# The first layer's front re-ordered: context loaded early, the sum with the summary made in TensorE's accumulators, constant transposes between short products, the one-hot table in halves

## The reference, cut to what matters

```python
def _L0_xattn_ref(Z, kv, decay, W_in, b_in, W_out, b_out, gamma, beta):
    K = jax.nn.sigmoid(decay)
    x = jnp.einsum('btd,ed->bte', kv, W_in) + b_in
    def scan_fn(s, xt):
        s = K * s + xt
        return (s, s)
    _, states = lax.scan(scan_fn, s0, jnp.swapaxes(x, 0, 1))
    proj = jnp.einsum('btd,ed->bte', states, W_out) + b_out
    summary = jnp.mean(proj, axis=1, keepdims=True)
    y = Z + summary
    return (y - mu) / jnp.sqrt(var + LN_EPS) * gamma + beta

x = x + _L0_xattn_ref(_layernorm(x), ctx_2048, ...)   # kv is (4, 64, 256)
x = x + _L0_ffn_ref(_layernorm(x), ...)               # 32 experts, 6 per token, 96 slots each
...
```

## Time and profile before

| | |
|---|---|
| median of 3 runs | 1086.76 us (1084.02 to 1087.8) |
| profiled execution, its own time | 1086.69 us |
| its span | 1085.4 us |
| PE busy | 949.7 us, 87% |
| DVE busy | 741.5 us, 68% |
| ACT busy | 637.0 us, 59% |
| POOL busy | 518.0 us, 48% |
| mean granted TensorE clock | 0.958 of full |

### The profile page before, as it was taken

One profiled execution on the slowest core, in us unless ns is written; L12 is line 12 of the kernel. 1 busy time (PEld: TensorE's weight loads), 2 busy tenths in 40 slices (PEclk: granted clock), 3 DMA queues, 4 the chain that ended last, 5 costly groups with the idle time before them and its releaser, 6 DMA issues.

```text
span 1085.4 us, 18121 instructions
## 1 busy us (share of the span) xinstructions
PE 949.7 (87%) x5833; PEld 786.0 (72%) x5833; DVE 741.5 (68%) x1996; ACT 637.0 (59%) x1816; POOL 518.0 (48%) x579
## 2 busy tenths in 40 slices
PE   6989871989987957599999999999999989997997
PEld 5776551565875756588898889888988778686785
DVE  6563222766664468689898989888888598668344
ACT  2655521020342537689898889989888663653353
POOL 1417773446544643255555555555443155543453
PEclk9789996999998989899999999999999999998999
DMA  9507987500036760020202020202000081005774
GB/s 386 190 18 210 219 212 191 152 1 0 2 137 219 252 218 1 1 64 2 64 2 64 2 63 2 64 1 64 14 13 2 1 251 28 1 1 214 240 272 164
DMA packets 57326, 108.57 MB, mean 100 GB/s; under 512 B 13648, under 2 KB 35280, under 8 KB 55312
## 3 DMA queue, kind: packets, MB, share of 16 engines
q1 hardware_dynamic: 47984, 89.42, 24.8%
q0 software_dynamic: 9248, 18.00, 6.4%
HBM read 78.67 MB, written 27.42 MB: 98 GB/s over the span
## 4 chain that ended last, share of the span: by engine, by line
PE 44%; DVE 19%; ACT 14%; DMA 8%; issue 7%; POOL 7%; SPq 1%; ACTq 0%; DVEq 0%; POOLq 0%
PE bank L201 22%; PE bank L210 7%; ACT a_p L3069 4%; DMA sum<-f_ys,f_index 4%; ACT a_p L3077 3%; PE bank L1338 3%; PE bank L2619 2%; PE bank L1872 2%; ACT a_qt L3052 2%; POOL f_xs L2190 2%; DVE a_qn L2828 2%; DVE stats L240 2%; ACT a_p L3019 1%; POOL sum L1199 1%; PE bank L2669 1%
## 5 line engine op out<-in xcount | busy, mean ns | idle before, releaser
L3196 POOL TENSOR_TENSOR a_p<-a_p,a_tot 128x128 f32<-128x128 f32 x64 | 50.6, 809 | 182.2 <-DVE a_tot L2800 182.2
L201 PE MATMUL bank<-a_w_high,a_in 128*128 128x256 f32 x384 | 99.1, 296 | 13.5 <-ACT a_p L3077 5.0
L210 PE MATMUL bank<-const 128*128 128x128 f32 x433 | 61.4, 300 | 43.1 <-DVE x L1111 21.4
L201 PE MATMUL bank<-a_w_low,a_in 128*128 128x256 f32 x384 | 94.8, 285 | 0.0
L210 PEld LDWEIGHTS bank<-const 128*128 128x128 f32 x433 | 55.8, 157 | 47.5 <-DVE x L1111 21.8
L201 PEld LDWEIGHTS bank<-a_w_high,a_in 128*128 128x128 f32 x384 | 74.1, 193 | 15.9 <-ACT a_p L3077 5.2
L3069 ACT ACTIVATE a_p<-bank,a_top 128x256 f32<-128x256 f32 x128 | 59.0, 477 | 31.0 <-DVE a_top L2852 28.6
L201 PEld LDWEIGHTS bank<-a_w_low,a_in 128*128 128x128 f32 x384 | 74.2, 193 | 0.0
L2852 DVE TENSOR_REDUCE a_top<-bank 128x2 f32<-128x512 f32 (+1 forms) x96 | 57.1, 601 | 20.3 <-PE bank L2619 15.6
L201 PE MATMUL bank<-cols,a_kv 128*128 128x256 f32 x256 | 61.9, 385 | 3.1 <-ACT a_kv L2992 3.1
L201 PE MATMUL bank<-a_proj_high,a_catq 128*128 128x256 f32 x256 | 62.5, 285 | 1.2 <-DVE a_catq L2247 0.8
(11 more groups left out here) (442 smaller groups left out, 3008.1 us busy)
## 6 DMA issues: line engine op xcount, KB each, us to landing
experts<-in_experts SPq DMA_DIRECT2D x49, 384.0 KB, 4.6
f_expert<-in_experts SPq DMA_DIRECT2D x31, 384.0 KB, 5.7
third_shelf<-in_groups SPq DMA_DIRECT2D x8, 1024.0 KB, 6.3
f_got<-f_xs SPq DMA_DIRECT2D x10, 516.0 KB, 8.0
third_shelf<-in_groups SPq DMA_DIRECT2D x8, 512.0 KB, 4.1
f_got<-f_ys SPq DMA_DIRECT2D x8, 512.0 KB, 5.2
f_xs<-blank_zero SPq DMA_DIRECT2D x1, 3999.0 KB, 21.6
l_expert<-in_experts SPq DMA_DIRECT2D x10, 384.0 KB, 7.7
```

The lines of the kernel that those rows point to most:

```text
L201: ins = pe.matmul(out, lhs, rhs, start=start and n == 0, stop=stop and n == len(pairs) - 1, skip_group_check=shared)
L210: ins = k.pe.transpose(o, i, ident[0:i.shape[0], 0:i.shape[0]])
L3196: g_.tensor_tensor(cross_probs(m, ti), cross_probs(m, ti), over(m.tot[n % 2][:, first:first + HPG], SC), ALU.mult).then_inc(*s["cross_weig ...
```

## The change

- *Loads.* SP's order becomes x, context, the first part of layer 0's weights (W_in, b_in, decay: 257.5 KB), const (710 KB), the rest of layer 0's weights, then as before. The column of -0.5 for POOL's powers is no longer loaded but set by POOL. POOL's iota and VectorE's statistics of x no longer wait for const.
- *TensorE in the first layer.* 18 products of a tile of zeros (`m.warm`) instead of 16 constant transposes; the normalised rows are put into banks 1, 2, 3 and 0 by products with the identity; the summary is made once as a 4x256 product (with b_out times 64), ScalarE scales it by 1/64 into SBUF, and eight products with a one-hot pick of the batch add it to the rows in the banks. 8, 6, 12 and 10 constant transposes stand between and behind.
- *VectorE in the first layer.* No widening, no addition of y; statistics and the first step of the update read the banks. Both additions of beta come after the scans.
- *Second layer.* TensorE waits for the statistics of half 0 of x (norm_var) instead of x itself, and runs 16 constant transposes there (with the 10 above: 26, where 28 were); 46 instead of 18 ahead of the picks; the picks wait for the half of the high table that they read. VectorE makes the facts and the high table, in halves, ahead of the weights.

```diff
-    on.wait_ge(*k.const_in)
-    pass_time(k, k.bank[7], 16)
-    on.wait_ge(*k.l0_in)
+    on.wait_ge(*s["warm_set"].at(1))
+    for _ in range(18):
+        pe.matmul(k.bank[7][:, 0:P], m.warm[:], m.warm[:], start=True, stop=True)
     on.wait_ge(*k.ctx_in)
+    on.wait_ge(*k.l0_first_in)
...
-    for b in range(B):
-        products(pe, k.bank[1 + b][:, 0:D], [(k.c["ones"][0:1, :], w["b_out"][0:1, :])], stop=False)
+    rows = rows_of(s)
+    on.wait_ge(*k.const_in)
+    for i in range(NT):
+        on.wait_ge(*rows[i][0])
+        if i // TPB == 3:
+            on.wait_ge(*s["seq_copied"].at(DC))
+        pe.matmul(y_part(k, i), k.c["ident"], k.rows[:, i, :], start=i % TPB == 0, stop=False, skip_group_check=True)
+    on.wait_ge(*k.l0_in)
+    summary = k.bank[SUMMARY_BANK][0:B, 0:D]
+    on.wait_ge(*s["picks_set"].at(1))
+    pe.matmul(summary, m.whole[:], w["b_out"][0:1, :], start=True, stop=False)
+    pass_time(k, k.bank[7], 8)
+    on.wait_ge(*s["keep_ready"].at(2))
+    for j in range(DC):
+        ins = pe.matmul(summary, m.mean_state[:, j, :], w_out[:, j, :], start=False, stop=j == DC - 1)
+    ins.then_inc(*s["summary_made"].one())
     layer1_compress_tensor(k, s)
-    pass_time(k, k.bank[7], 10)
-    on.wait_ge(*s["keep_ready"].at(2))
-    for b in range(B):
-        products(pe, k.bank[1 + b][:, 0:D], [(m.mean_wide[:, j * B + b, :], w_out[:, j, :]) for j in range(DC)],
-                 start=False).then_inc(*s["summary_made"].one())
-    layer1_values_tensor(k, s, [k.kvc_copied.at(1), s["y_added"].at(NT)])
+    on.wait_ge(*s["picks_set"].at(2))
+    on.wait_ge(*s["summary_copied"].at(1))
+    for i in range(NT):
+        if i == HALF:
+            pass_time(k, k.bank[7], 6)
+        pe.matmul(y_part(k, i), m.picks[:, i // TPB, :], m.summary[:], start=False, stop=True,
+                  skip_group_check=True).then_inc(*s["y_made"].one())
+    pass_time(k, k.bank[7], 12)
+    layer1_values_tensor(k, s, [k.kvc_copied.at(1), s["summary_copied"].at(1)])
+    on.wait_ge(*s["x_added"].at(NT))
+    pass_time(k, k.bank[0], 10)
...
 def layer0_ffn_tensor(k, m, s):
     pe, on = k.pe, k.on_pe
-    for r in k.x_ready[NT - 1]:
-        on.wait_ge(*r)
-    pass_time(k, k.bank[0], 28)
+    on.wait_ge(*s["norm_var"].at(2))
+    pass_time(k, k.bank[0], 16)
     turn_rows_tensor(k, s, k.rows, rows_of(s))
...
-    pass_time(k, k.bank[1], 18)
-    on.wait_ge(*s["hot_ready"].at(2))
+    pass_time(k, k.bank[1], 46)
     counts = k.bank[1][0:CAP, :].rearrange("p (c n) -> p c n", c=OF)
     for i in range(NT):
+        on.wait_ge(*s["hot_ready"].at(2 + i // HALF))
         on.wait_ge(*s["facts_scaled"].at(i + 1))
...
-    v.tensor_tensor(m.high_hot, middle(by_eight(m.high), HIGH), around(m.highs), ALU.is_equal).then_inc(
-        *s["hot_ready"].one())
+    for half in range(NT // HALF):
+        part = slice(half * HALF * OF, (half + 1) * HALF * OF)
+        v.tensor_tensor(m.high_hot[:, part], middle(by_eight(m.high)[:, part, :], HIGH), around(m.highs, HALF * OF),
+                        ALU.is_equal).then_inc(*s["hot_ready"].one())
...
         x_in = k.load("x_in", k.x[:], a["x"])
+        k.ctx_in = k.load("ctx_in", ctxt[:], a["ctx"])
+        first = width(L0A[:3])
+        k.l0_first_in = k.load("l3_context_in", l0[:, 0:first], a["l0"][:, 0:first])
         k.const_in = k.load("const_in", const[:], a["const"])
-        k.l0_in = k.load("l0_in", l0[:], a["l0"])
-        k.ctx_in = k.load("ctx_in", ctxt[:], a["ctx"])
+        k.l0_in = k.load("l0_in", l0[:, first:width(L0A)], a["l0"][:, first:width(L0A)])
```

More of the change, by code:

```diff
@@ L646, in layer0_attention_vector @@
     v.tensor_reduce(m.mean_state[:].rearrange("p j b -> p (j b)"),
[L647 to L650, removed]
+                    m.states[:].rearrange("p j (b t) -> p (j b) t", b=B), AX.X, ALU.add).then_inc(
+        *s["keep_ready"].one())
+    on.wait_ge(*k.l0_in)
+    add_beta(0)
     add_beta(1)
-    y_ready = [[s["y_added"].at(i + 1)] for i in range(NT)]
     for half in range(NT // HALF):
[L654 to L660, removed]
+        tiles = range(half * HALF, (half + 1) * HALF)
+        for i in tiles:
+            on.wait_ge(*s["y_made"].at((i // TPB + 1) * TPB))
+            ins = v.bn_stats(k.moments[half].stats[:, i % HALF, :], y_part(k, i))
+        ins.then_inc(*step.one())
+        gathered_moments_vector(k, k.moments[half], HALF, s2["norm_var"])
     for half in range(NT // HALF):
@@ L684, in layer0_attention_scalar @@
                      bias=w["b_in"][:, i:i + 1]).then_inc(*s["seq_copied"].one())
+    norm_rows_scalar(k, s, 1, k.x, k.rows, k.x_ready)
+    on.wait_ge(*s["summary_made"].at(1))
+    a.activation(m.summary[:], k.bank[SUMMARY_BANK][0:B, 0:D], ACT.Copy, scale=1.0 / SC).then_inc(
+        *s["summary_copied"].one())
     layer1_compress_scalar(k, s)
@@ L690, in layer0_attention_pool @@
     g, on, step, w = k.g, k.on_g, k.g_step, k.l0
-    on.wait_ge(*k.const_in)
+    g.memset(m.warm[:], 0.0).then_inc(*s["warm_set"].one())
+    g.memset(k.minus_half[:], -0.5).then_inc(*step.one())
+    g.memset(m.whole[:], float(SC)).then_inc(*s["picks_set"].one())
+    on.wait_ge(*step.now())
     k.g.iota(k.keys[:], [[1, SC]], base=0, channel_multiplier=0,
@@ L694, in layer0_attention_pool @@
     normalise_pool(k, s, k.x, k.rows, k.x_ready)
+    on.wait_ge(*k.const_in)
+    g.tensor_copy(m.picks[:], over(k.c["ident"][0:B, 0:B], P)).then_inc(*s["picks_set"].one())
     for half in range(NT // HALF):
@@ L1058, in layer0_ffn_vector @@
     by_eight = lambda tile: tile[:].rearrange("p (n e) -> p n e", e=LOW)
-    middle = lambda ap, n: ap.unsqueeze(2).broadcast_to([P, NT * OF, n, LOW])
-    around = lambda tile: tile[:].unsqueeze(1).broadcast_to([P, NT * OF, tile.shape[1], LOW])
+    middle = lambda ap, n: ap.unsqueeze(2).broadcast_to([P, ap.shape[1], n, LOW])
+    around = lambda tile, n=NT * OF: tile[:].unsqueeze(1).broadcast_to([P, n, tile.shape[1], LOW])
     v.tensor_tensor(m.low_hot, middle(by_eight(m.low), LOW), around(m.lows), ALU.is_equal).then_inc(
         *s["hot_ready"].one())
+    on.wait_ge(*s["hot_ready"].now())
+    v.tensor_scalar(m.facts[:, :, 0, :, :].rearrange("p n l e -> p n (l e)"), m.low_hot.rearrange("p n l e -> p n (l e)"),
+                    c["tokpart"], float(NT), ALU.mult, ALU.mult).then_inc(*step.one())
+    for half in range(NT // HALF):
+        part = slice(half * HALF * OF, (half + 1) * HALF * OF)
+        v.tensor_tensor(m.high_hot[:, part], middle(by_eight(m.high)[:, part, :], HIGH), around(m.highs, HALF * OF),
+                        ALU.is_equal).then_inc(*s["hot_ready"].one())
     v.reciprocal(m.total[:], m.total[:]).then_inc(*step.one())
@@ L3227, in layer2_attention_pool @@
     on.wait_ge(*step.now())
[L3228 removed]
+    g_.tensor_tensor(k.l3_krms[:], k.l3_kms[:], k.minus_half[:, 0:CTX // P], ALU.pow).then_inc(*step.one())
     on.wait_ge(*step.now())
@@ L3874, in constants @@
         "slot1": (TOK + 1 + part)[:, None], "tokpart": (part + 1)[:, None],
-        "eighth": (part // 8 * 8)[:, None], "in_eighth": (part % 8)[:, None],
-        "minus_half": np.full((P, 16), -0.5)})
+        "eighth": (part // 8 * 8)[:, None], "in_eighth": (part % 8)[:, None]})
 def swap_halves(w):
```

42 lines of the change are left out of this document (23 added, 19 removed).

## The result

The changed kernel takes **1100.22 us** (median of 4 runs, 1095.81 to 1103.16), the kernel before 1085.66 on the same chip (4 runs, 1084.02 to 1087.8): a ratio of **1.0133, with an interval of 1.0095 to 1.0171**. It is slower. The forecast was 1079.5, and even the rival on the slow side gave only 1090.0. The profiled execution took 1101.36 us with a span of 1100.1, 14.7 more than the span before, and TensorE's mean granted clock fell from 0.958 to 0.943.

A forecast was written before the change was run, and what follows sets the result against it. Bound taken: engines taking turns, none full, and TensorE at half clock after two gaps. Front -1.9, gate -3.2, keys and mask -0.3, index picks -1.8: -7.2 us from 1086.69 gives 1079.5, range 1076.5 to 1083.6.

The forecast's parts named there:

- the rival on the slow side: Ahead of the index table's picks: 46 constant transposes at half clock become the wait, +5.2 us there; total 1090.0; chance 0.04.
- the value products start near 23.5 ... 0.8 later: TensorE's queue in the front: after 16 picks (3.7 us) and transposes, values start near 23.5 instead of 22.67.
- the step after it that moved their end along by 0.8: Value products end at 36.9 instead of 36.1, ScalarE's copies at 38.4; row transposes start at 40.0 instead of 41.5, -1.5.
- the clock falls already in the front: Idle TensorE between 9 and 11.9 puts identity products at half clock, +1.7 us; total 1081.2; chance 0.25.
- The rival of the hole behind the fold: Fold at full clock leaves 2 us before the keys; half of them run at half clock, +1.7; total 1080.9; chance 0.10.
- The gap ahead of the row transposes: TensorE idle 39.3 to 41.5; without it, full clock expected in row transposes and gate, gate -3.2 us.
- x's statistics at 5.6: VectorE's statistics of x in the first layer start at 5.6 instead of 7.75.
- the gate near full speed: Gate product, 32 records: 3.7 us instead of 6.9, -3.2; bounds 0 and -3.4.
- the picks of the index table: One-hot table picks at full clock: 2.0 us, end 71.9 instead of 73.7, -1.8; bounds -0.4 and -2.2.
- x not late for anything: Update of x ready 3.8 us earlier, most of that gain hidden behind the value products.
- Cost nothing: Index weights ready 2.5 us later, their write still ahead of the first gather's index; up to 0.5 us if late.
- what lies behind the index moves along: Everything after the index table follows the earlier index, since no transfer is issued at a fixed time.

The follow-up runs named there:

- experiment 1: Changed kernel, summary-adding products with 128 rows (124 of them zero) instead of 4: 1115.22 us, ratio to the kernel before 1.002.
- experiment 2: Kernel before, 12 products into an unread bank added ahead of the value products: 1138.23 us with 4 rows, 1125.2 with 128 (one run each).
- experiment 3: Kernel before with only the second layer's edits (46 transposes, facts before weights, high table in halves): 1106.38 us, ratio to the kernel before 0.9937.
- experiment 5: Changed kernel, 12 constant transposes ahead of the values dropped (with 128-row summary products): 1108.03 us; or made 52 (4-row products): 1117.35 us.
- experiment 6: 16 constant transposes added between fold and keys; ratios to before: changed kernel with 128-row products 0.9982, also without the 12 0.9962, second-layer edits alone 0.9993.

## Why the prediction was wrong, and where it was right

**The step that failed** is the sentence on TensorE's queue, "the value products start near 23.5 ... 0.8 later", with the step after it that moved their end along by 0.8. It takes 16 records of picks at full clock and the values as they were. The first eight picks are as reckoned; during the second eight the clock fell, and the values took 24.4 us instead of 13.4. (The terms themselves, 17.0 + 0.9 + 3.7 + 0.7 + 1.4, add up to 23.7 and not 23.5; with full rows the values started at 24.00.) In numbers: -7.2 forecast at the gather, +8.1 measured, and experiment 1, which changes the rows alone, gives -7.4 (68.70 - 76.13).

**The rival "the clock falls already in the front" was named, but wrong in two ways.** Its cause was idle time between 9 and 11.9; that gap (0.99 and 0.58 us in the changed kernel) brought no fall in any trace, and the fall came at 21.7, in work without a gap. And its price, +1.7, supposed that the clock would come back within 3 us, as in the second stretch of rows 2. It didn't: the values ran their 24.4 us at 0.50 in the changed kernel and 24.3 in experiment 2. So a fall can cost the whole stretch behind it. That supposition was the false one: I took the recovery as a property of the clock and not of the work behind it.

**Why the values and the keys don't raise the clock is not shown.** My expectations said: because they are paced by another engine. The traces don't bear this out. At 0.50 TensorE is busy for 24.40 of 24.40 us and ScalarE waits for it; the keys take 7.14 us for 32 records at 1.00, which is 0.223 a record and no more than the 0.232 of the summary products ahead of the values (3.72 us / 16), so even there nothing holds them up. Two rivals were not tried. TensorE loads weights in only 13.96 of the 24.40 us, and in 8.74 of 13.80 for the slow keys, but in 6.00 of 6.00 for the transposes that raised the clock. And the keys' operands have 64 rows, as have those of a third of the values' records (L498), so the rows of experiments 1 and 2 could be at work here too. Nor is the state fixed by the start: in the second trace of the changed kernel the values began at 0.50 and were at 1.00 after 1 us, and the keys of the kernel before began at 0.50 and took 7.39.

**The rival of the hole behind the fold** was right that the hole brings a fall, and mis-sized in the same way: 1.7 reckoned; 13.28 and 13.96 us instead of 7.39, so about 6. It didn't come in the changed kernel, where the fold ran at half clock and left no hole.

**The gap ahead of the row transposes** was taken for what halved the gate's clock. That is half right: the gap of 2.2 us stands in four traces, and the clock fell right behind it in two of them (experiment 3). Without the gap the gate took 3.73 to 4.47 us, but the clock still fell in the gate or the fold in most of those traces (59.2 in the changed kernel, 46.0 in experiment 1).

**The slow rival** (transposes as the new wait) fell: 46 took 5.22, within the 4.9 to 5.3 reckoned. Constant transposes ran at 1.00 and raised the clock in experiment 5 (30.8, after 5.9 us of them and nothing else), and in the changed kernel it rose 1.2 us into them (52.3), against the rule of the Trainium skill (TensorE: Matmul & The Clock Gate, Part 4, PE-mode transpose) that the full clock doesn't engage with them.

**Right:** x's statistics at 5.6 (5.59); the gate near full speed (4.46 for 32 and, in experiment 1, 3.73, for 3.7 reckoned); the picks of the index table 1.95 for 2.0; x not late for anything. "Cost nothing" for the late weights held in the changed kernel (the gather waits for the index), but not where the index is early: 1.3 us in experiment 3, against a bound of 0.5.

**That what lies behind the index moves along** was half right. The 8.1 us of loss stood 200 us later as 8.5. Of the gains less was left.

**Still open:** what the changed kernel loses behind the first experts: 1.3 us in small steps between 310 and 850 (the lag is 9.2 at 344 and 9.5 at 480), 3.3 us behind 970, beside a fall of the clock that the other profile lacks there, and 1.6 us behind TensorE's last products. Such stretches differ by execution in all kernels, and one trace for each doesn't tell chance from cause. What the waits on "remote" are couldn't be tried with a kernel.

## What to carry to other kernels

A product with few rows saves no time and can cost TensorE its clock: eight records took 1.99 us with 4 rows and with 128, and 128, most of them zero, kept it at 1.00, so here a small operand was better padded with zeros. Price a fall of the clock by what runs behind it, and look that up in traces at both levels: constant transposes brought it back after 5.9 us in experiment 5, while the values stayed at 0.50 for all of their 24 us in two traces and the slow keys for 13 in two. Ahead of such a stretch check in the profile that TensorE has no hole and full operands; that a short filler in a hole holds the clock is shown by one trace (experiment 6).

## What the hardware showed that I hadn't expected

- The granted clock fell from 1.00 to 0.50 while TensorE was busy all the time: at 21.7 in the changed kernel and at 25.7 with 12 products of 4 rows in the kernel before; with 128 rows in these products it stayed at 1.00. It also fell in or behind the gate's products of 32 columns and 128 rows (46.0 in experiment 1, busy 2.00 of 2.00 us ahead of it), though not in every trace.
- Rows of zeros were enough: in experiment 1, 124 of the 128 rows are zero, and the clock held.
- The same stretch has two lasting speeds: 13.4 and 24.3 to 24.4 us for the values, 7.14 and 13.28 to 13.96 us for the keys.
- One program took both ways on two executions: values at half clock and first gather at 84.22, or at full clock and 71.80. The fall came 1.4 us later in the second; that this made the difference is likely, not shown.
